# Attention's rows normalised on the way through PE, by diagonals that POOL makes, instead of by ACT

## The reference, cut to what matters

```
query = ctx @ Wq.T + bq ;  key = ctx @ Wk.T + bk          # 256 tokens x 128, for each batch
energy = query @ key.T                                     # 256 x 256
attention = softmax(energy, axis=-1)                       # rows divided by their sums
x = x + tanh(g_xattn[0]) * einsum("bln,bmn->blm", layernorm(x), attention)
```

## Time and profile before

| what | value |
|---|---|
| median of three runs | 416.19 us (413.0 to 417.19) |
| the profiled execution | 413.12 us |
| its span, first to last instruction | 411.3 us |
| PE, DVE, ACT, POOL busy | 82%, 74%, 64%, 63% of the span |
| mean granted clock of PE | 0.922 of full speed |
| first attention around the change | 34 to 58 us of the span |

### The profile page before, as it was taken

How to read it: one execution, slowest core, us unless ns; L and a number is a source line. 1 busy time by engine, 2 the same in 40 slices (tenths; PEclk the granted TensorE clock), 3 DMA queues, 4 the chain that set the end, 5 groups by cost and what they waited for, 6 DMA issues and landing times.

```text
span 411.3 us, 7575 instructions
## 1 busy us (share of the span) xinstructions
PE 337.9 (82%) x2217; PEld 267.8 (65%) x2217; DVE 305.8 (74%) x696; ACT 263.2 (64%) x530; POOL 259.5 (63%) x213
## 2 busy tenths in 40 slices
PE   4944974598789789989885189999999999999990
PEld 2431663256566567666685078899998997998870
DVE  2999889979999999999898956544554535354456
ACT  0899999999888898888273445445445444444410
POOL 4200013689996897788423487887887787878740
PEclk9995895599999989989999579999999999999997
DMA  7930430477343877441198438899899888864558
GB/s 222 374 132 0 130 127 13 156 248 245 121 153 121 281 262 253 160 138 67 36 249 204 117 112 205 227 204 233 212 237 225 211 222 202 221 146 101 90 91 268
DMA packets 59132, 72.17 MB, mean 175 GB/s; under 512 B 6802, under 2 KB 43458, under 8 KB 59106
## 3 DMA queue, kind: packets, MB, share of 16 engines
q1 hardware_dynamic: 49104, 56.04, 43.8%
q0 software_dynamic: 8832, 15.74, 19.1%
q10 hardware_dynamic: 1170, 0.08, 0.2%
HBM read 61.75 MB, written 10.09 MB: 175 GB/s over the span
## 4 chain that ended last, share of the span: by engine, by line
PE 38%; ACT 24%; DMA 14%; DVE 14%; issue 6%; POOL 2%; SPq 2%; DVEq 0%; POOLq 0%; ACTq 0%
PE bank L1328 12%; PE bank L1366 9%; PE bank L1321 6%; ACT ssm L862 4%; PE bank L1308 3%; DVE bank L1565 3%; DMA B_last<-bc_rows 3%; DMA ssm<-bc_rows 3%; PE bank L1162 3%; DMA arena<-in_L_ffn_w_gate_up 3%; ACT L862 3%; DMA ssm<-routed,idx 3%; ACT L900 2%; DVE ssm L1570 2%; PE bank L1314 1%
## 5 line engine op out<-in xcount | busy, mean ns | idle before, releaser
L602 POOL TENSOR_TENSOR ssm<-ssm,arena 128x1024 f32<-128x1024 f32 x31 | 73.1, 2359 | 18.7 <-DVE ssm L1570 9.5
L1570 DVE TENSOR_TENSOR_SCAN ssm<-ssm,bank 128x512 f32<-128x512 f32 x64 | 78.1, 1221 | 4.2 <-issue 2.0
L675 POOL DMA_INDIRECT ssm<-routed,idx x64 | 65.2, 1019 | 21.8 <-issue 14.6
L1795 DVE SCALAR_TENSOR_TENSOR ssm<-ssm,bank 128x96 f32<-128x96 f32 x64 | 20.1, 313 | 75.8 <-ACT ssm L974 75.6
L686 POOL DMA_INDIRECT sums<-ssm,idx x40 | 65.3, 1633 | 13.5 <-issue 10.4
L1328 PE MATMUL bank<-ssm,wguT 128*128 128x256 bf16 x576 | 72.4, 272 | 0.1
L1328 PEld LDWEIGHTS bank<-ssm,wguT 128*128 128x128 bf16 x576 | 56.1, 98 | 12.0 <-DVE ssm L1787 0.5
L974 ACT ACTIVATE ssm<-bank 128x96 f32<-128x96 f32 x64 | 16.0, 250 | 74.0 <-PE bank L1366 74.0
L1162 PE MATMUL bank<-xs,wguT 128*128 128x512 bf16 x192 | 48.5, 406 | 7.9 <-POOL xs L589 4.2
L1366 PE MATMUL bank<-arena,ssm 128*128 (+1 forms) x256 | 53.3, 331 | 1.6 <-ACT ssm L957 1.1
L862 ACT ACTIVATE ssm<-delta,A_sb 128x510 f32<-128x510 f32 x64 | 43.9, 714 | 6.1 <-DVE ssm L1570 5.9
(11 more groups left out here) (227 smaller groups left out, 667.5 us busy)
## 6 DMA issues: line engine op xcount, KB each, us to landing
ssm<-bc_rows SPq DMA_DIRECT2D x22, 512.0 KB, 3.6
arena<-bc_rows SPq DMA_DIRECT2D x16, 512.0 KB, 5.0
arena<-in_L_ffn_gate_proj SPq DMA_DIRECT2D x32, 192.0 KB
arena<-in_L_ffn_up_proj SPq DMA_DIRECT2D x32, 192.0 KB
arena<-in_L_ffn_down_proj SPq DMA_DIRECT2D x32, 192.0 KB
B_last<-bc_rows SPq DMA_DIRECT2D x10, 512.0 KB, 3.6
sums<-zero_f SPq DMA_DIRECT2D x1, 2304.0 KB, 14.0
arena<-in_L_ffn_w_gate_up SPq DMA_DIRECT2D x1, 2048.0 KB, 11.7
```

Source lines behind the costliest of these rows:

```text
L602: pool.tensor_tensor(prod[:, a:b, :], hs[:, a:b, :], C_all[:, 2 * (q % 8):2 * (q % 8) + 2, :], ALU.mult).then_inc(s.prod_ok, 1)
L675: pool.indirect_dma_start(out=xe[:, k, :], out_offset=None, in_=routed, in_offset=bass.IndirectOffsetOnAxis(ap=idx2[:, k, 0:1], axis=0)).t ...
L1570: dve.tensor_tensor_scan(hs[:, k % 4, :], dA[:, k % 3, :], x[:, :], 0.0, ALU.mult, ALU.add).then_inc(s.scan_ok, 1)
```

## The change

ACT's eight scaled copies are gone. POOL, behind `ln_rstd(1)`, waits for the reciprocals and makes eight diagonal matrices: the identity times the reciprocal of each row's sum (`att_diag`, in a part of `wpT` that is free then). PE's turn becomes an ordinary f32 product of the undivided rows with that diagonal, which turns and divides in one. The semaphore `att_n` is now raised by POOL.

```diff
         xdbl = part(wpT[0:XR, 0, 0:1], (1, TOK))
+        att_diag = part(wpT[:, 0, 0:1], (P, NT), (1, P), offset=TOK)
...
             ln_rstd(1)
 
+            pool.wait_ge(s.att_r, 1)
+            for j in range(NT):
+                pool.tensor_tensor(att_diag[:, j, :], ident[:, :], part(rasum[:, j:j + 1], (0, P)), ALU.mult).then_inc(s.att_n, 1)
+
             ln_rstd(2)
...
             for c in range(2):
-                for j in range(4 * c, 4 * c + 4):
-                    act.wait_ge(s.att_r, 1)
-                    act.activation(att[:, j, :], att[:, j, :], ACT.Copy, scale=rasum[:, j:j + 1]).then_inc(s.att_n, 1)
                 act.wait_ge(s.xd_ps, c + 1)
                 act.activation(xdbl[:, c * 512:(c + 1) * 512], bank[5 + c][0:XR, :], ACT.Copy).then_inc(s.xd_sb, 1)
...
                         pe.wait_ge(s.att_n, 2 * b + qh + 1)
-                        ins = pe.transpose(bank[1 + b][:, kh * L + qh * P:kh * L + qh * P + P], att[:, 2 * b + qh, kh * P:kh * P + P], ident[:, :])
+                        ins = pe.matmul(bank[1 + b][:, kh * L + qh * P:kh * L + qh * P + P], att[:, 2 * b + qh, kh * P:kh * P + P], att_diag[:, 2 * b + qh, :],
+                                        start=True, stop=True)
```

## The result

The changed kernel takes 427.24 us (median of four, 426.53 to 429.0) against 414.99 (four runs of the kernel before): 12.25 us more. The ratio estimated from the single runs is 1.0306 (95% interval 1.0262 to 1.035); the quotient of the two medians is 1.0295. The profiled execution has the highest time of the four (429.0, span 427.0), while that of before (413.12) is near the lowest of its own, so the two traces differ by 15.7 us of span: 12.64 at the first scan of the state stage (73.46 and 86.10 us), 14.63 at its last (200.13 and 214.76), the rest behind it, in stages that the change does not touch. I compare the traces only up to the third x1, where the change's effect is complete.

The account below looks back on a forecast made before the run. ACT's gapless chain was taken to bound the kernel; alternating POOL and DVE make diagonal 7, then half-clock PE, late, 13.1 less 0.31 giving 12.8 us. Sum 425.9 or 429.0, forecast 427.5 us; range 413 to 430.

Parts of the forecast that it names:

- POOL and DVE exclude each other, one for one: In the quantisation, POOL's diagonals and DVE's SBUF steps alternate whole instructions; chain 12.8 us late, chance 0.62.
- The rival that POOL runs its eight in a row: POOL makes all diagonals from 37.1 to 39.7 us; DVE some 1 us late, 414 to 417 us; chance 0.16.
- The rival that the diagonals meet nothing: POOL's eight are done before 41.5 us; 0.6 us gained, 412.5 to 415.6 us; chance 0.15.
- What a turn of POOL costs: In the quantisation, 0.3 us of POOL between any two DVE steps; diagonal 7 there at 52.2 us.
- the base: Sum is 425.9 us on the profiled 413.1, 429.0 on the median 416.2; 427.5 put between them.
- PE's queue and its clock: L1067 and L1074 queue behind diagonal 7; PE at half clock, L1067 taking 6.8 us; full clock leaves 7.2 us late.
- The rule of the Trainium skill (SBUF — State Buffer, Who interferes with whom): VectorE's second read port and GpSimd's only one are one lock, held a whole instruction by whichever starts first.
- The figure of the Trainium skill (TensorE: Matmul & The Clock Gate, Terms): Transpose mode makes f32 four times as fast; PE's 16 products would take some 7 us, 5 us later.
- ACT's prize of 0.6 us: ACT sheds eight copies, 3.19 us, but `xdbl` waits for PE, so the signs start only about 0.6 us earlier.
- PE's product and the clock behind it: Turns cost 1.6 us more, L1074 starts 1.1 us later; steadier clock worth up to 1.6; cancelling, bad end 0.8 late.
- the lateness passes to the end undiminished: From the third x1 the chain runs on DVE, ACT and PE without load; the 12.8 us pass to the end.

Follow-up runs that it names:

- one: Changed kernel, but POOL makes all eight diagonals in one instruction of 1024 columns instead of eight instructions: ratio 1.0 to the kernel before.
- two-each: Changed kernel, but POOL makes two diagonals with each of four instructions of 256 columns: ratio 0.9976 to the kernel before.
- waiting: Changed kernel, but DVE does not begin the quantisation until POOL's eight diagonals are made: ratio 1.0013 to the kernel before.
- delta first: Changed kernel with the products for `delta` put ahead of the turning products on PE: ratio 1.0104 to the kernel before.
- DVE kernels: Changed kernel, but DVE makes the eight diagonals in one f32 product of 1024 columns and POOL makes nothing: ratio 0.9997 to the kernel before.
- product-alone: Kernel before (ACT divides, POOL makes nothing) with PE's turns replaced by ordinary f32 products with the identity: ratio 0.9998 to the kernel before.
- filled: Changed kernel with 23 products of zeros on PE where it waits for diagonals 4 to 7: ratio 1.0188 to the kernel before.
- warm: Kernel with two diagonals per POOL instruction, plus 40 products of zeros on PE ahead of the products for `xdbl`: ratio 1.0007 to the kernel before.
- unused-diagonals: Kernel before, ACT's copies and PE's turns kept, with POOL also making the eight diagonals for no one: ratio 1.0002 to the kernel before.

## Why the prediction was right

It was right in sign, in mechanism and in size: 427.5 us foretold, 427.24 measured. By its steps:

- POOL and DVE exclude each other, one for one: shown, by the trace of the changed kernel (eight products ended by eight steps) and by the one, two-each and waiting kernels, where the loss goes with the number of meetings. The rival that POOL runs its eight in a row is refuted by the trace; its price, 1 us, is what such a row costs when it is forced (+0.81 where DVE waits). The rival that the diagonals meet nothing is refuted by the same rows.
- What a turn of POOL costs: mis-sized, and made up for elsewhere. I put 0.3 us between two steps of DVE, and each engine was to wait for the other's whole instruction. POOL did, but DVE lost less than POOL's product takes alone (0.36 us): its first six steps took 11.07 us from start to end instead of 10.29 (34.69 to 45.76 and 34.83 to 45.12), 0.16 for each of the five turns between them. So diagonal 7 came 16.25 us behind the reciprocal's start, not 17.5 (52.2 less 34.72). PE took that back: the last products 1.65 us for 1.3, L1070 7.12 for 6.8, the first half of L1077 5.85 (59.66 to 65.51) for 5.2. Second pair of x1: 65.6 foretold, 65.51 measured; lateness on the way to the third x1: 12.8 foretold, 12.78 measured. An error of 1.3 us on either side, and the closeness of the sum owes something to that. It owes something to the base too: I put it halfway between 413.1 and 416.2 us, at 414.7, and the four runs of the kernel before have a median of 414.99. The runs can't tell 12.8 us from 11 or 14: the interval of the ratio is some 10.9 to 14.5 us.
- PE's queue and its clock: right. The order of the queue is worth 7.85 us (delta first), the clock 3.04 where zeros keep it up to the last diagonal. The two overlap, since a PE at full clock also shortens the queue.
- The rule of the Trainium skill (SBUF — State Buffer, Who interferes with whom), which I set beside the rows, holds in these runs as far as the two exclude each other: 2.90 us alone, 15.98 beside DVE. That the lock is held for a whole instruction fits DVE's steps, which POOL waited out, and not POOL's products, of which DVE lost 0.16 us for 0.36. The order of the turns, which it leaves open, came from the earlier trace rows, and they had it right. The figure of the Trainium skill (TensorE: Matmul & The Clock Gate, Terms), by which PE would have been 5 us later, is not borne out: 3.84 against 1.97 us.
- ACT's prize of 0.6 us: the signs start 7.58 us behind the reciprocal instead of 8.00, and 7.33 with two each. ACT could use 0.4 to 0.7 of its 3.2 us. In the changed kernel this was of no use to anyone.
- PE's product and the clock behind it: taken as cancelling, with 0.8 us as the bad end. In the one-instruction, waiting, two-each and DVE kernels the clock held over the products with x (7.17 us), and the way is 0.27 us shorter to 0.81 us longer, the longest where DVE waits 3 us; in the product-alone kernel it fell, and the way is 1.03 us longer, a little past my bad end.
- That the lateness passes to the end undiminished: right for the median (12.25). The profiled execution shows 3 us more, gathered in the scan's stage and behind it; the two executions lie at opposite ends of their kernels' runs, and what makes these 3 us is open.

## What to carry to other kernels

An engine that is idle in the profile is not free if its neighbour runs two-input steps on SBUF: look at the pair, and count the meetings ahead of whoever waits for the result, not the work. Give POOL few large instructions there (one of 1024 columns cost nothing measurable, eight of 128 cost 12 us, and the same eight cost nothing where no one waited for them). A late result costs what is queued behind its waiter, so put work that doesn't need it ahead of the wait: that alone gave back 7.85 of 12.78 us here.

## What was not expected of the hardware

DVE lost less to POOL in a meeting than POOL's product takes by itself. A turn of 128 columns (0.36 us alone) cost DVE 0.16 us; one of 256 columns 0.29 to 0.41 (0.61 alone), by which the steps were longer; one of 1024 columns 1.58 (2.36 beside DVE's steps with an input in PSUM). Either POOL does a part of its work before its turn, or it lets DVE go early; the runs don't tell which.

PE's clock fell while PE was busy without a gap. In the kernel before this came during the last of the 8-row products for `delta` (0.89 in 46 to 47 us, 0.50 in 47 to 48; L1067 ends at 47.33), and not behind them, as the prediction reads the earlier trace rows. In the filled, the warm and the delta-first kernel it came during these products too, though in the first two full-size products ran right ahead of them; in the unused-diagonals and the product-alone kernel it came up to 1 us behind them. In four kernels (one instruction, two each, DVE waits, diagonals by DVE) it held over the same order of work. The two-each and the product-alone kernel even have turning products and products for `delta` of the same length (3.84 and 3.69 us), and the clock held in one and fell in the other. What decides is open.
